# A four-layer transformer kernel on one core: the first projections, the last quad and the start of the sparse layer in another order

## What is computed

```
x = layernorm(x + polynomial_attention(x))     # 16 heads, degree 4
x = layernorm(x + sorted_ffn(x))               # 2 experts, one per token
x = layernorm(x + softmax_attention(x))        # 32 heads of 8, causal, rotated twice, biases
x = layernorm(x + routed(x) + shared(x))       # 32 experts

# last layer
scores = sigmoid(x @ gate_w)
topk_w, topk_i = top_k(scores, 6);  topk_w /= sum(topk_w)
routed = sum over the 6: topk_w * (silu(x @ wg[e]) * (x @ wu[e])) @ wd[e]   # 256 -> 96 -> 256
shared = silu(x @ sg) * (x @ su) @ sd                                       # 256 -> 192 -> 256
```

## Time and profile before

| | us |
|---|---|
| median of 3 runs | 1681.36 (1674.04 to 1687.87) |
| the profiled execution, device time | 1682.43 |
| its span | 1680.7 |
| PE / DVE / ACT / POOL busy | 1372.8 / 1084.3 / 829.4 / 570.6 |
| chain that ended last: PE / DVE / ACT / POOL | 59% / 23% / 7% / 5% |
| mean granted clock of PE | 0.875 of full |

### The profile page before, as it was taken

The page is one execution under the profiler, slowest core; times in us unless marked ns, Lnnn a source line. Parts: engine busy times, 40 slices in busy tenths (PEclk is TensorE's granted clock), DMA queues, the critical chain, the costliest instruction groups (busy, mean ns, idle before and its releaser), DMA issues.

```text
span 1680.7 us, 27081 instructions
## 1 busy us (share of the span) xinstructions
PE 1372.8 (82%) x10128; PEld 886.8 (53%) x10128; DVE 1084.3 (65%) x2291; ACT 829.4 (49%) x1211; POOL 570.6 (34%) x674
## 2 busy tenths in 40 slices
PE   5377746675689999589999899889999687999982
PEld 4233443342478877344554555444554254799971
DVE  7678795867453354567777566667767536455676
ACT  2467525655342342126666345466667332366660
POOL 7477343547201104101011000001110375766661
PEclk9599975987798999659999899789999777999996
DMA  2690000002211101000000000000001337577875
GB/s 87 209 353 33 1 1 1 1 1 88 78 35 63 39 14 36 7 1 1 1 2 2 1 1 1 1 1 2 2 1 64 113 134 260 179 209 210 262 262 204
DMA packets 69077, 124.36 MB, mean 74 GB/s; under 512 B 7318, under 2 KB 55126, under 8 KB 67928
## 3 DMA queue, kind: packets, MB, share of 16 engines
q1 hardware_dynamic: 56664, 85.92, 15.9%
q0 software_dynamic: 12288, 36.72, 5.9%
HBM read 60.22 MB, written 62.39 MB: 73 GB/s over the span
## 4 chain that ended last, share of the span: by engine, by line
PE 59%; DVE 23%; ACT 7%; POOL 5%; issue 3%; DMA 1%; POOLq 0%; SPq 0%; DVEq 0%; ACTq 0%
PE psum L2269 10%; PE psum L2142 9%; PE psum L2242 6%; PE psum L2452 6%; DVE probs L2823 5%; PE psum L2359 4%; PE psum L2202 4%; DVE neg_max L2805 4%; PE psum L2475 3%; PE psum L2219 3%; PE psum L2380 3%; PE psum L335 3%; ACT probs L2565 2%; POOL probs L3354 2%; PE psum L2163 2%
## 5 line engine op out<-in xcount | busy, mean ns | idle before, releaser
L2565 ACT ACTIVATE probs<-psum 128x1024 f32<-128x1024 f32 (+1 forms) x480 | 437.2, 945 | 280.3 <-PE psum L2256 153.6
L2805 DVE TENSOR_REDUCE neg_max<-psum 128x1 f32<-128x512 f32 (+3 forms) x768 | 380.0, 551 | 130.9 <-PE psum L2219 115.0
L2242 PE MATMUL psum<-qt,kt 32*128 32x512 f32 (+6 forms) x1152 | 244.2, 456 | 26.2 <-ACT probs L2565 9.9
L2269 PE MATMUL psum<-probs,v 128*32 128x256 f32 (+3 forms) x2048 | 185.9, 451 | 56.6 <-POOL probs L3354 42.9
L2823 DVE TENSOR_TENSOR probs<-probs 128x1024 f32<-128x1024 f32 (+1 forms) x152 | 200.2, 1375 | 44.2 <-ACT probs L2565 43.7
L2202 PE MATMUL psum<-kt,qt 32*128 32x512 f32 (+3 forms) x768 | 203.0, 453 | 26.4 <-DVE neg_max L2805 24.8
L2242 PEld LDWEIGHTS psum<-qt,kt 32*128 32x128 f32 (+1 forms) x1152 | 108.9, 198 | 189.7 <-issue 100.1
L340 POOL TENSOR_SCALAR q_rows<-neg_max 128x16 fp32r<-128x16 f32 x32 | 7.1, 221 | 553.2 <-DVE neg_max L2813 362.1
L3423 POOL DMA_INDIRECT results<-sp_y,sp_row x128 | 124.8, 975 | 59.1 <-ACT sp_y L2620 32.5
L2142 PE MATMUL psum<-ident,q_rows 128*128 128x128 f32 x384 | 69.8, 327 | 67.4 <-ACT k_rows L2494 52.0
L2202 PEld LDWEIGHTS psum<-kt,qt 32*128 32x128 f32 x768 | 95.2, 196 | 52.7 <-DVE neg_max L2805 45.4
(11 more groups left out here) (323 smaller groups left out, 2613.8 us busy)
## 6 DMA issues: line engine op xcount, KB each, us to landing
many_x<-blank SPq DMA_DIRECT2D x2, 10240.0 KB, 50.9
sp_xs<-many_x SPq DMA_DIRECT2D x64, 320.0 KB, 3.5
sp_w<-in_sparse SPq DMA_DIRECT2D x8, 1280.0 KB, 10.0
x_turned<-results SPq DMA_DIRECT2D x8, 768.0 KB, 7.0
sp_back<-results SPq DMA_DIRECT2D x8, 768.0 KB, 9.2
sorted_x<-blank SPq DMA_DIRECT2D x2, 1152.0 KB, 6.5
sorted_y<-y SPq DMA_DIRECT2D x18, 128.0 KB, 1.7
rows<-in_x SPq DMA_DIRECT2D x4, 512.0 KB, 6.9
```

What stands on the lines that cost most here:

```text
L2242: inst = pe.matmul(psum[:, base - early:base + QCH - q0], A.kt[rows, k_slot, key * P:(key + 1) * P], A.qt[rows, q_slot, c * QCH + q0 - ear ...
L2269: inst = pe.matmul(psum[32 * h:32 * h + 32, bank + q0:bank + q1], A.v_of(b)[:, key, col:col + 32], A.probs[:, slot, h, at:at + q1 - q0], s ...
L2565: act.activation(dst, view, ACT.Exp if A.softmax else ACT.Square).then_inc(exped.by(A.layer, b, quad, c, step, h0), 1)
L2805: inst = dve.tensor_reduce(A.neg_max[:, g % 2, 0 if last else 1, tile, h0 + i:h0 + i + 1], bank[:, at * P:(at + cols) * P], X_AXIS, ALU.ma ...
```

## The change

Three things are moved, and one buffer with them.

1. `attention_setup` of ACT and DVE becomes `weights_cut` and stands in the sorted layer, two blocks from its end. The eight projections run in one row without `max_unit`s in between; the first half is cut after projection 3; `combine` and `moments` of the last sorted batch stand between the projections 4 to 7; `root`, `moments`, `root` of the two halves stand between the maxima, and both `scale`s in the first quad.
2. In the last quad `experts` moves from place 0.7 to 5, in plan order behind `normalize` (2.5); the shared weights are loaded in it and the first shared gates run at 6.4; the output of the first half is normalized, turned and projected 0.5 to 1.5 places earlier, its norm follows at 7.1 to 9.1, and the tokens of part 1 are turned at 9.4 and 9.7.
3. `amid_last` becomes a generator whose pieces stand among the last weights: `logits` ahead of them, `score` behind, then `pick`, and `rank`, `slots`, all 24 scatters of part 1 and the shared gates (0, 1) ahead of the last projection. Tokens turned for the router are kept (`x_turned` is now two buffers; the first batch's lies in the place of `sp_xs`, the buffer of the fetched pairs), so the 24 transposes fall away, and the first four `bring_pair` wait for the shared gates (1, 1).

```diff
                 for t in range(HALF):
+                    project(0, t)
+                    gathers[t]()
+                cut(0, 0, HALF, hurry=True)
+                project(0, HALF)
+                sums[0]()
+                project(0, HALF + 1)
+                turn(0, 0, HALF)
+                moments[0]()
+                project(0, HALF + 2)
+                sums[1]()
+                project(0, HALF + 3)
+                units = max_units(FIRST_PLANS)
...
-                return places + [(0.7, lambda: route["experts"](take_single, give_single)), (2.3, bring)]
+                places += [(2.3, bring), (5, lambda: route["experts"](take_single, give_single)), (6.4, first_shared)]
+                return places + [(9.4, lambda: turn_third(0)), (9.7, lambda: turn_third(2))]
...
-                        between += [(5.5, lambda: normalize_half(b, 0)), (7, lambda: turn_out(b, 0)), (8.5, lambda: project_out(b, 0))]
-                        if b == BATCH - 1:
-                            between.append((9.9, norm))
+                        between += [(5, lambda: normalize_half(1, 0)), (6, lambda: turn_out(1, 0)), (7, lambda: project_out(1, 0)),
+                                    (7.1, lambda: early.extend(plan_norm(norms_due.pop(0)))), (7.5, lambda: early[0]()),
+                                    (9, lambda: early[1]()), (9.1, lambda: early[2]())] if b else [
...
+                ending = amid()
+                next(ending)
                 while due:
                     weigh()
+                next(ending)
                 normalize_half(1, 1)
+                next(ending)
                 turn_out(1, 1)
                 unwound = fence()
-                amid()
+                next(ending)
                 project_out(1, 1)
...
-                route1["rank"](take, give)
                 for part in route["turn"]:
-                    part(take, give)
...
-                for t in range(0, TILES, 2):
-                    turn_shared(0, t)
-                for t in range(0, HALF, 2):
-                    turn_shared(1, t)
...
+                for p in range(4):
+                    bring_pair(p, ((hidden, ml, "shared", 1, 1, "up"),))
```

278 lines of the change are left out of this document (140 added, 138 removed).

## The result

Eleven runs each, in the same sitting: the changed kernel takes 1670.4 us (1666.01 to 1682.58), the kernel before 1683.48 us (1674.04 to 1690.31). The ratio is 0.9936, 95% interval 0.9918 to 0.9954: 10.8 us less, where I had forecast 24.4. By my own bound of 1% that is no change. The profiled execution took 1666.9 us, its span is 1665.2.

A forecast was written before the change was run, and what follows sets the result against it. PE's waits and low clock were taken to bound, with POOL's scatters deciding pair 8; 1682.43 - 12.3 (second attention's start) - 12.0 (last quad to pair 8) = 1658.1 us, 1657.0 against the median; range 1645 to 1671.

The forecast's parts named there:

- (a): Start of the second attention: with the weights' cut in the sorted layer, the first projection starts 1.1 us earlier.
- (b): First projection of the second attention: shorter PE pause, it may stay at full clock; gain 0 to 1.5 us, 0.7 taken.
- (c): Second attention, fourth projection's rotation to first exponential: 45.2 us become 32.9 or 32.7; gain 12.3, 12.5 kept.
- (d): First quad: the two `scale`s come back there and cost 2 us, between nothing and 3.3 us.
- The rival with the better clock: First quad: denser projections carry the full clock into it, 8.8 us more won, 1648 us; chance 0.12.
- The first term: Start of the second attention: 1.1 + 0.7 + 12.5 - 2.0 = 12.3 us won.
- PE's wait for `best`: Last quad: of PE's wait of 12.15 us for `best` 10.0 are won, the rest becomes a wait for `ao`.
- POOL's 96 scatters run without a gap.: Last quad to pair 8: part 1's `where` starts at 1380.9 us, needed at 1386.8; scatters end at 1447.5, 13.3 earlier.
- I get the first pairs at about 1425 us, 25 earlier.: Behind the last quad: transposes gone (5 us), two shared steps' gates earlier (7 to 11), norm about 6 us earlier.
- PE waits 10 us at pair 8 and comes back at the low clock, 3.0.: Pair 8: PE arrives before POOL's rows, waits about 10 us, then loses 3.0 us at half speed.
- Three table loads at nothing.: Last quad and behind it: ACT gets 31 table loads for 28, 3.8 us in all, costed at nothing.
- one term only: Rival, 1668 us, chance 0.28: part 1's `where` too late (1669), or the start only moves work (1667).

The follow-up runs named there:

- e13: The changed kernel itself, run again without a further edit as measure beside later runs; ratio 0.9906 to the kernel before.
- the start alone: The kernel before with only the change's first part (weights' cut in the sorted layer, projections in one row, scales in the first quad); ratio 0.9944.
- own columns and early products: The changed kernel with `where` columns for both batches and `shared_mult` ahead of `slots`, `experts`, `shared_add`; ratio 0.9828, on slow chips 0.9833 and 0.9821.
- early products: The changed kernel with only `shared_mult` put ahead of `slots`, `experts` and `shared_add`; ratio 0.9883, on slow chips 0.9828 and 0.9814.

## Why the prediction was right and wrong, step by step

*What bounds.* Right: both places at which the gain was looked for are places where PE waits. That POOL's and PE's clocks both run towards pair 8 was right too, but I took the wrong one for the slower.

*(a), (b), the first projection.* From the transposes to its start 3.44 us against 4.45 (657.27 - 652.82): 1.0 won, forecast 1.1. Its own time fell too, from 3.63 us at a granted clock of 0.59 (657.27 to 660.90) to 2.32 us at 1.00 (654.91 to 657.23).

*(c), the 45.2 us to the first exponential.* 668.49 to 700.23 is 31.7 us, forecast 32.7 to 32.9. Right, and so was the way to it: the groups of DVE's operations and the idle time that the order leaves.

*(d), the scales in the first quad.* From the transposes the first exponential comes 16.0 us earlier, the output copy in the second quad 13.3: 2.6 us were given back, forecast 2.0 with bounds 0 and 3.3. The number was right by luck. From the first exponential to that copy PE's idle time is 5.1 us, before 5.4; what grew is its busy time for the same work, 64.5 us for 61.6, at a granted clock of 0.63 for 0.68. And the second trace of the same kernel (e13), with the same scales in the same place, took 66.5 us for it, less than the kernel before with its 67.0 (at a clock of 0.68):

```profile
700.23:769.89 69.66, 64.52 (x430) 32.39 (x429) 47.49 (x101) 28.56 (x32) 6.29 (x23) 0.63 0.00 1
```

```profile
705.84:772.35 66.51, 60.37 (x430) 30.01 (x429) 47.44 (x101) 28.54 (x32) 6.27 (x23) 0.71 0.00 1
```

So the price was the clock's and not the scales', which cost at most the 0.7 us by which PE's idle time in e13 is above that of the kernel before. The rival with the better clock didn't come: up to about 750 us the granted clock was 0.50.

*The first term:* 13.3 us in this trace and 16.5 in the second, forecast 12.3; by the ratio of the start alone 9.4 us with an interval of 4.5 to 14. Right in size, with (d) for another reason.

*PE's wait for `best`.* From the mask's matmul to the scores behind the wait 12.5 us (1298.01 to 1310.50) against 22.4 (1335.93 - 1313.52): 9.9 won, forecast 10.0. Right.

*"POOL's 96 scatters run without a gap."* **This step failed.** The chain to `where` itself was sized right: ready 69.6 us behind the mask's matmul, forecast 67.4. What I left out, that is put at nothing, is the wait that stands in `many_slots` ahead of it. I had read in the trace of before that `where` came late, and made it early; I did not ask what the early `where` would meet. The code names the landing, and the trace of before bounds it: SP's fetch, which waits for it, was issued at 1388.08, 74.6 us behind the mask's matmul, 7 us behind my forecast for `where`. Measured was 80.4 (1378.40 - 1298.01): the landing took 8.3 us from the scatter's start, with the experts' fetches, which the change moves ahead, issued 8.4 us before that; in the trace of before, where they come behind it, 2.5 us. The rule of the rival, that each us of a late `where` opens POOL's gap by one, held (8.3 us), but with a price that I put in the wrong place: the gap cost nothing where PE wasn't ahead at pair 8 (0.9882 with it, 0.9881 without), DVE's queue 6 to 8 us.

*"I get the first pairs at about 1425 us, 25 earlier."* **This step failed too, and worse.** 111.5 us behind the mask's matmul was forecast, 137.1 measured, and 121.0 with both waits gone. I counted 7 to 11 us for shared gates that are "earlier": but they are earlier inside the same stretch of PE, and work moved within it wins nothing. Only the 24 transposes leave it, which took 3.43 + 1.19 = 4.6 us. And I didn't weigh the line of the diff that halves the banks. In the groups of PE's instructions from the end of the `best` or `ao` wait to the first pairs, before:

```profile
L2402 PE MATMUL psum<-shared_down,s_hid 96*128 96x256 f32 x64 | 15.1, 381 | 1.9 <-DVE s_hid L3095 1.9
L2392 PE MATMUL psum<-x_turned,shared_gate 128*96 128x512 f32 x32 | 15.1, 593 | 0.0
L2392 PE MATMUL psum<-x_turned,shared_up 128*96 128x512 f32 x32 | 15.0, 592 | 0.0
```

and after:

```profile
L2416 PE MATMUL psum<-shared_down,s_hid 96*128 96x256 f32 x64 | 17.0, 415 | 8.2 <-DVE s_hid L3109 8.2
L2406 PE MATMUL psum<-sp_xs,shared_gate 128*96 128x512 f32 x16 | 10.6, 801 | 0.0
...
L2406 PE MATMUL psum<-x_turned,shared_gate 128*96 128x512 f32 x16 | 8.7, 670 | 8.2 <-DVE s_hid L3109 8.2
L2406 PE MATMUL psum<-x_turned,shared_up 128*96 128x512 f32 x16 | 8.3, 646 | 0.0
...
L2406 PE MATMUL psum<-sp_xs,shared_up 128*96 128x512 f32 x16 | 7.5, 592 | 0.0
```

The same 128 matmuls cost 52.1 us instead of 45.2, and these 6.9 us are more than the 24 transposes gave. Little of it goes away with the waits: with own columns and early products, where the wait of 8.15 us and two of the three others are gone, the 128 still cost 50.0 us. Three places make up the sum. Behind the wait of 8.15 us eight `shared_down` take 3.78 us at a granted clock of 0.50; at 1419.14 us, at 1.00, eight take 1.89. Behind that of 3.92 the gates take 2.88 and 2.69, at 1417.42, at 1.00, four take 1.88; behind 2.37 and 1.91 us they take 1.96, nearly as at the full clock. The rest, 3.0 us, is in two groups of gates that follow the router's logits and their short waits, PE:

```profile
1359.36 3.53 PE L2406 MATMUL psum<-sp_xs,shared_gate 128*96 128x512 f32 x4
...
1390.70 3.24 PE L2406 MATMUL psum<-sp_xs,shared_gate 128*96 128x512 f32 x4
```

The granted clock was 0.50 from 1348.5 to 1359.3 and 0.54 from 1371.2 to 1390.7. In the kernel before, the first transposes stood behind the second logits and were slow in the gates' place: 16 took 3.43 us at a granted clock of 0.57, at 652.82 us and 1.00 they took 1.94. So what follows the logits ran at a low clock in both traces (behind the first ones it was the output projection before, at 0.50 from 1379.9 to 1384.0), and without the transposes it is the gates that pay.

*PE waits 10 us at pair 8 and comes back at the low clock, 3.0.* It did neither; it waited nowhere there, as it was 26 us later than forecast.

*From the last scatter to pair 8, 3.4 and 3.5 us.* In the one kernel in which POOL binds, from the scatter's end 1436.91 - 1430.30 = 6.6. Right.

*Three table loads at nothing.* Right as far as the rows show. One of those in the new ending and the instruction behind it, ACT:

```profile
1360.43 1.28 ACT L2642 ACT_TABLE_LOAD   x1
1362.93 0.59 ACT L2642 ACTIVATE s_silu<-psum 96x512 f32<-96x512 f32 x1 [1.21 <-PE psum L2406]
```

ACT still waits 1.21 us for PE behind the load, so that this one cost PE nothing. One load, which both kernels have, is on PE's path in the new place: that ahead of the root of the first half's norm (1341.37 to 1342.65), behind which DVE scales the `rows` for which PE waits 2.59 us. The trace has 31 loads of 1.28 us, that of before 28.

*Behind pair 8 nothing changes.* Right (though 18.63 us over eight pairs is 2.33, not 2.82; 2.82 us is the steady spacing of later pairs): from the first to the last pair 178.18 us against 178.15, from there to the end 51.95 against 51.79.

*The sum and the chances.* 12.3 came as 13.3, 12.0 as 0.2. What happened is the rival "one term only", with its cause (part 1's `where` too late) and its 1669 us. I gave it 0.28. Two signs of being wrong that I had named came: the gap on POOL, and pair 8 turned 15.7 us earlier than 1469 while PE did not wait for it. The rival deserved more, as its condition had only been looked at from one side: I had worked out when DVE would be ready, not what else `where` needs.

## What to carry to other kernels

When a write is moved earlier, list every wait in front of it, also those that the trace shows at zero: they were free because it was late. Ask which instructions stand behind such a wait on the same engine; here they cost more than what it guards, and it was enough to put the wait on another engine. When a transfer is moved earlier, ask whose landing it will run beside. Work moved within one engine's stretch wins nothing by itself, and one row moved alone (`experts`) was worth more than a rebuilt ending that has it too, but queues more work behind DVE's waits. That halving the banks costs by itself was not run alone: it is read from the code and from the waits that the early products shorten.

## What I had not expected of the hardware

The same program had two speeds by chip: the kernel before took about 1683 us on some and 1801 to 1810 us on three others. On these three the stretch from the mask's matmul to the first pairs takes 194 to 221 us instead of 121 to 139, and from the first to the last pair 206 to 215 instead of 178 to 180; everything before is alike (from the first exponential to the mask's matmul 592.9 to 607.5 us). Own columns and early products on such a chip, PE and then ACT:

```profile
1354.90 0.79 PE L2256 MATMUL psum<-qt,kt 32*128 32x512 f32 x2 [19.06 <-ACT probs L2579]
1380.70 0.79 PE L2256 MATMUL psum<-qt,kt 32*128 32x512 f32 x2 [17.93 <-DVE xt L2714]
```

```profile
1353.82 1.02 ACT L2579 ACTIVATE probs<-psum 128x1024 f32<-128x1024 f32 x1 [20.01 <-issue]
1378.37 1.02 ACT L2508 ACTIVATE xt<-psum 128x1024 fp32r<-128x1024 f32 x1 [23.52 <-remote]
```

ACT stands for 20.0 and 23.5 us with no releaser that the trace can name, and PE behind it. Both slow stretches are those in which POOL issues scatters, in the last quad at its usual 1.27 us each. What holds ACT there no run of this study shows. The ratios to the kernel before were alike on both kinds of chip for two of the three kernels that ran on both, and for the early products alone lower on the slow ones (0.9828 and 0.9814 against 0.9883).
